# Cross-attention layer 0: probabilities cross PSUM two heads at a time over two adjacent banks, one bank for outputs, one for the rest, scaling on POOL, queries reloaded by batch

## The chip, the core and the metric

One NeuronCore of a Trainium2 chip runs the whole program; the metric is the device time of one launch in microseconds (us). Engines work from their own in-order queues and meet only at semaphores: TensorE (PE, with its weight loads PEld), VectorE (DVE), ScalarE (ACT), GpSimd (POOL) and SyncE (SP), whose queue here only issues DMAs.

## The reference, cut to what matters

Two layers follow each other on 8 batches of 112 tokens with a context of 375 rows; the change touches only the attention of the first layer, L0.

```python
def L0(x, ctx, mask):                       # x (8,112,512), ctx (8,375,512)
    q = (x @ Wq + bq)                       # 32 query heads of 16
    k, v = ctx @ Wk + bk, ctx @ Wv + bv     # 8 key/value heads of 16
    scores = q_head @ k_head.T / 4 + mask   # 112 x 375 for each (batch, query head)
    attn = softmax(scores)
    out = attn @ v_head                     # 112 x 16
    x = out @ Wo + bo + x
    return layernorm(x) * gamma + beta
# L1: two cross attentions (16 heads of 128), each with a layernorm and an output projection, then an MLP
```

## The kernel before

The batches are done in two halves of four (loop variable `hf`). A half is: a preparation (context and queries split in a high and a low fp32r part, keys, values and the first queries projected), the L0 attention, its output projection and layernorm, then eight groups of L1 attention and an MLP. In L1 every product is three matmuls (hi·hi, hi·lo, lo·hi; L652 to L654), and these fill most of the time.

**The L0 loop** runs over `n` = 0 to 127 heads of a half: `c` (four chunks of eight heads), in it `b` (four batches), in it eight heads. Step `n` writes these instructions on each engine:
- PE: three transposes of head `n`'s weights into a PSUM bank (`transpose0`, L784, recorded at L657), the scores of head `n+4` (`scores0`, L779), in some steps the projection of keys or queries (`L0_AT`), and for four heads together (a quad) six matmuls weights · values (`weigh0`, L802 to L805), the transposes of a finished quad (`four_transpose0`) and of a finished batch (`out_transpose0`).
- DVE: `max0(n+4)` (L1483: scores + mask to SBUF and their row maximum), then `lo_of` (L1318): transposed weights in PSUM minus their high part, 125x336, for head `n`; per quad `sum_outputs` (L1491, L1492); per eight heads (an octet) `scale_outputs` (L1499: 112x128, divides by the softmax sums) and `out0` (L1320).
- ACT: `move` (L1011) of the transposed weights of head `n` out of PSUM, rounded to the high part; `exps0(n+3)` (L1117); per quad `outputs` (33x448); per octet `out0` (L1013).

PSUM has eight banks. In L0 the loop uses two `scores`, two `tp` for transposes (by head, `n % 2`), `o_ps` and `pj2` for outputs (by quad), `pj0` and `pj1` (`aux`) in turn for everything else. `tp_free`, counted by `lo_of`, gates transpose `n+2`; `o_mid` gates the outputs bank; `aux_free` the aux banks.

**Queries and keys** pass through DRAM. Chunk `c+1`'s queries (448 columns, all four batches) replace chunk `c`'s in the tile `qo` by two DMAs of 64 partitions (`load_queries0(c, kv)`), each allowed only when the last heads that read its rows have been scored: after step 28 and 32 of the 32 heads of the chunk. Keys are reloaded batch by batch. The raw weights of the output projection and of L1's first group are loaded by SP between these and split on POOL in one piece, ahead of nothing else there.

## Time and profile before

| what | value |
|---|---|
| median of three runs (lowest, highest) | 2555.87 us (2555.66, 2564.72) |
| the profiled execution, its span | 2556.51 us, 2554.7 us |
| busy in the span: PE, PEld, DVE, ACT, POOL | 91%, 81%, 59%, 39%, 27% |
| L0 loop of half 0: first to last `max0` | 77.6 to 228.6 us |
| L0 loop of half 1: first to last `max0` | 1340.7 to 1489.8 us |
| granted TensorE clock, mean | 0.97 of full |

A row of the time line gives the start, the duration, engine, line and shapes of an instruction and, in brackets, how long the engine had idled and what released it. Durations overlap the next instruction's start, so the cost of an instruction in a stream is the step to the next start. A row of a table by stretch gives the stretch, its length and each engine's busy time in it.

### The profile page before, as it was taken

The numbers are of one execution on the slowest core, as the hardware profiler recorded it, in microseconds if no ns is written. First come the engines' busy times: TensorE is split into PE (matmuls) and PEld (weight loads), VectorE is DVE, ScalarE is ACT, GpSimd is POOL, SyncE is SP. The second block draws the span as 40 slices with busy tenths as digits, with TensorE's granted clock in tenths as the row PEclk, the third lists the DMA queues.
The fourth block names the chain that finished last, engine by engine and source line by source line (L and its number), as shares of the span: only waits on it lengthen the run. The fifth ranks groups of instructions, "written<-read, shape, count | busy, mean of one in ns | idle before, by whom it ended". The sixth has DMA issues, their size and how long they took to land. (4 is left out here: it accounts for less than half of the span.)

```text
span 2554.7 us, 36666 instructions
## 1 busy us (share of the span) xinstructions
PE 2329.4 (91%) x13176; PEld 2077.3 (81%) x13176; DVE 1506.3 (59%) x3426; ACT 998.7 (39%) x2271; POOL 698.1 (27%) x734
## 2 busy tenths in 40 slices
PE   4798799999999999998969978999999999999988
PEld 4565698999989898997756657999889898998976
DVE  4697655455575555456538976455555655455564
ACT  2686333332434333243118843342424333242420
POOL 4021213224141313313541211214141313314045
PEclk8899899999999999999989988999999999999999
DMA  5632222232333323223453412232323223223222
GB/s 184 203 113 61 66 87 92 88 103 84 104 99 92 100 75 104 88 91 127 149 160 103 111 49 68 90 95 88 102 94 102 92 79 103 86 91 116 77 69 81
DMA packets 118889, 253.25 MB, mean 99 GB/s; under 512 B 13648, under 2 KB 37232, under 8 KB 117664
## 3 DMA queue, kind: packets, MB, share of 16 engines
q1 hardware_dynamic: 76504, 140.73, 17.9%
q10 hardware_dynamic: 42208, 110.18, 14.0%
q8 instruction: 109, 1.79, 0.3%
q14 instruction: 68, 0.56, 0.1%
HBM read 222.40 MB, written 31.22 MB: 99 GB/s over the span
## 5 line engine op out<-in xcount | busy, mean ns | idle before, releaser
L652 PE MATMUL pj<-ctx_hi,wk_hi 128*128 128x376 f32 x1088 | 380.3, 350 | 36.5 <-DVE xacc L1369 21.6
L653 PE MATMUL pj<-ctx_lo,wk_hi 128*128 128x376 f32 x1088 | 372.7, 343 | 0.0
L654 PE MATMUL pj<-ctx_hi,wk_lo 128*128 128x376 f32 x1088 | 371.5, 341 | 0.0
L1318 DVE TENSOR_TENSOR rr<-pj,rr 128x448 fp32r<-128x448 f32 (+1 forms) x280 | 174.4, 628 | 249.5 <-ACT rr L1011 249.5
L576 POOL TENSOR_SCALAR wk_hi<-raw 128x512 fp32r<-128x512 f32 (+1 forms) x84 | 52.5, 625 | 977.6 <-DMA raw<-in_wk 817.8
L1320 DVE SCALAR_TENSOR_TENSOR k_lo<-pj,cur,k_hi 128x375 fp32r<-128x375 f32 x256 | 155.1, 607 | 247.2 <-ACT k_hi L1013 245.9
L657 PEld LDWEIGHTS tp<-ident,probs 112*125 112x125 f32 (+1 forms) x1536 | 197.9, 165 | 120.4 <-DVE probs L1598 41.9
L652 PE MATMUL pj<-pt_hi,nat 125*128 125x448 f32 x768 | 287.0, 374 | 7.0 <-issue 5.9
L657 PE MATMUL tp<-ident,probs 112*125 112x112 f32 (+1 forms) x1536 | 231.6, 270 | 60.2 <-DVE probs L1598 36.0
L1195 ACT ACTIVATE probs<-scores,prm 112x376 f32<-112x376 f32 x256 | 147.4, 576 | 353.2 <-DVE prm L1590 353.1
L1013 ACT ACTIVATE k_hi<-pj,cur 128x375 fp32r<-128x375 f32 x256 | 146.8, 573 | 353.1 <-PE pj L654 343.3
L654 PE MATMUL pj<-pt_hi,nat 125*128 125x448 f32 x768 | 282.5, 368 | 0.0
L653 PE MATMUL pj<-pt_lo,nat 125*128 125x448 f32 x768 | 282.2, 367 | 0.0
L652 PEld LDWEIGHTS pj<-ctx_hi,wk_hi 128*128 128x128 f32 x1088 | 211.4, 194 | 41.0 <-DVE xacc L1369 23.4
L576 POOL TENSOR_SCALAR wb_hi<-raw 128x512 fp32r<-128x512 f32 x152 | 98.1, 645 | 474.9 <-ACTq L1221 185.3
L1011 ACT ACTIVATE rr<-pj 128x448 fp32r<-128x448 f32 (+1 forms) x280 | 152.3, 547 | 162.0 <-PE pj L654 152.2
L653 PEld LDWEIGHTS pj<-ctx_lo,wk_hi 128*128 128x128 f32 x1088 | 211.3, 194 | 1.2
L654 PEld LDWEIGHTS pj<-ctx_hi,wk_lo 128*128 128x128 f32 x1088 | 210.8, 194 | 0.0
L578 POOL TENSOR_TENSOR wb_lo<-raw,wb_hi 128x512 fp32r<-128x512 f32 x152 | 200.6, 1320 | 12.7
L1318 DVE TENSOR_TENSOR pt_lo<-tp,pt_hi 126x336 fp32r<-126x336 f32 (+1 forms) x384 | 181.3, 500 | 10.0 <-ACT pt_hi L1011 10.0
L1011 ACT ACTIVATE pt_hi<-tp 126x336 fp32r<-126x336 f32 (+1 forms) x384 | 157.8, 448 | 46.6 <-PE tp L657 45.7
L652 PEld LDWEIGHTS pj<-pt_hi,nat 125*128 125x128 f32 x768 | 144.2, 188 | 27.5 <-issue 16.4
(168 smaller groups left out, 5326.9 us busy)
## 6 DMA issues: line engine op xcount, KB each, us to landing
nat<-nat_scratch ACTq DMA_DIRECT2D x256, 384.0 KB, 3.7
raw<-in_wk SPq DMA_DIRECT2D x72, 256.0 KB, 3.8
raw<-in_wq SPq DMA_DIRECT2D x72, 256.0 KB, 3.3
raw<-in_wo SPq DMA_DIRECT2D x72, 256.0 KB, 2.6
raw<-in_wv SPq DMA_DIRECT2D x64, 256.0 KB, 3.3
raw<-in_w SPq DMA_DIRECT2D x64, 256.0 KB, 2.9
nat_scratch<-rr SPq DMA_DIRECT2D x8, 1536.0 KB, 7.0
queries_scratch<-rr SPq DMA_DIRECT2D x32, 224.0 KB
```

The lines of the kernel that those rows point to most:

```text
L576: nc.gpsimd.tensor_scalar(hi, src, 1.0, 0.0, ALU.mult, ALU.add).then_inc(split_hi, 1)
L578: nc.gpsimd.tensor_tensor(lo, src, hi.bitcast(F32), ALU.subtract).then_inc(signal, k)
L652: nc.tensor.matmul(dst, l_hi, r_hi, start=first, stop=False)
L653: nc.tensor.matmul(dst, l_hi, r_lo, start=False, stop=False)
L654: return nc.tensor.matmul(dst, l_lo, r_hi, start=False, stop=last)
L657: return nc.tensor.transpose(dst, src, ident[0:parts, 0:parts])
L1011: i = nc.scalar.activation(dst, src, ACT.Copy)
L1013: i = nc.scalar.activation(dst, src, ACT.Identity, bias=bias)
L1195: nc.scalar.activation(probs[0:L, h, 0:SK], scores[n % SCR][0:L, 0:SK], ACT.Exp, bias=neg_max[0:L, h:h + 1], accum_out=row_sum[0:L, h:h + ...
L1318: i = nc.vector.tensor_tensor(dst, src, hi.bitcast(F32), ALU.subtract)
L1320: i = nc.vector.scalar_tensor_tensor(dst, src, bias, hi.bitcast(F32), ALU.add, ALU.subtract)
```

## The change

- **Two heads at once.** `tp0` and `tp1` become one tensor `tp_two` of two adjacent banks, `pj0` and `pj1` become `pj_two`. Heads are paired: the six transposes of a pair fill both banks of one of these (pairs take them in turn), then one `move` of 125x672 on ACT and one `lo_of` of 125x672 on DVE take both. New semaphores `two_ready`, `two_mid`, `two_free` count pairs; a pair's transposes wait for `lo_of` of the pair before the last.
- **Fewer banks for the rest.** Outputs have `o_ps` alone (`outputs` moves ahead of the `move` on ACT, and `weigh0` waits for `o_mid` of the quad before), all else has `pj2` alone.
- **Scaling on POOL.** `scale_outputs` leaves DVE for POOL; POOL's splits of the next weights are put between the scalings by twos, and their loads on SP move accordingly, with the copy of the second half's context now behind the four loads of `wo0`.
- **Queries by batch.** A chunk's queries come in eight DMAs of 64x4x112, two per batch, each pair as soon as the batch's heads of the chunk before are scored. `L0_AT` moves: keys 3 from step 9 to 5, queries from 15, 47, 79 to 12, 44, 76, in two steps instead of four.

```diff
-L0_AT = {1: ("k", 2), 9: ("k", 3), 15: ("q", 1), 47: ("q", 2), 79: ("q", 3)}
+L0_AT = {1: ("k", 2), 5: ("k", 3), 12: ("q", 1), 44: ("q", 2), 76: ("q", 3)}
-        o_banks, aux = (o_ps, pj[PJ - 1]), pj[0:NAUX]
+        twos, aux = (tp_two, pj_two), pj2
...
-                def load_queries0(c, kv):
-                    sp.wait_ge(q0_out, (hf * C0 + c + 1) * 64)
+                def load_queries0(c, b):
+                    if b == 0:
+                        sp.wait_ge(q0_out, (hf * C0 + c + 1) * 64)
                     if c > 0:
-                        sp.wait_ge(sc_ready, hf * SC_H + c * HB * HPC - 4 * (KV2 - 1 - kv))
+                        sp.wait_ge(sc_ready, hf * SC_H + (c - 1) * HB * HPC + (b + 1) * HPC)
+                    for kv in range(KV2):
+                        sp.dma_start(qo[64 * kv:64 * kv + 64, 4 * kv:4 * kv + 4, cols].bitcast(F32),
+                                     q_dram[hf, c, 4 * kv:4 * kv + 4, :, :, :, cols].rearrange("j r e d t -> (r e d) j t")
+                                     ).then_inc(q0_in[b], 16)
...
+                for i in range(NT // 8):
+                    scale_outputs(hf, i)
+                    if i in (3, 4):
+                        weights(base + RAW_W0, "o", hf * WO_H, hf * WO_H, chunks=range(2 * i - 6, 2 * i - 4))
+                    if i in (7, 8):
+                        keys1(0, range(2 * i - 14, 2 * i - 12))
+                    if i in (9, 10):
+                        queries1(0, chunks=range(2 * i - 18, 2 * i - 16))
...
                 def transpose0(n):
+                    two, i = divmod(n, 2)
                     pe.wait_ge(exp_ready, sc0 + n + 1 + SCR)
-                    pe.wait_ge(tp_free, tp0 + n + 1)
+                    if i == 0 and two >= 2:
+                        pe.wait_ge(two_free, two0 + two - 1)
...
-                        pe.wait_ge(tp_free, tp0 + 4 * u + 4 + TP)
-                        if u > 1:
-                            pe.wait_ge(o_mid, o0 + u - 1)
+                        pe.wait_ge(two_free, two0 + 2 * u + 2)
+                        if u > 0:
+                            pe.wait_ge(o_mid, o0 + u)
...
-                    move(pt0[n // 4 % 2][0][0:KC, n % 4, :], tp[n % TP][0:KC, 0:SC * L], tp_ready,
-                         tp0 + n + 1, mid=tp_mid)
+                    if n >= 8 and n % 4 == 0:
+                        outputs((n - 8) // 4)
+                    if n % 2 == 1:
+                        move(pt0[n // 4 % 2][0][0:KC, n % 4 - 1:n % 4 + 1, :], twos[two % 2][0:KC, :, 0:SC * L],
+                             two_ready, two0 + two + 1, mid=two_mid)
                     if n + 3 < NT:
                         exps0(n + 3)
-                    if n >= 8 and n % 4 == 0:
-                        outputs((n - 8) // 4)
...
-                        if n % 8 == 6:
-                            scale_outputs((n - 14) // 8)
```

On DVE, in the middle of the loop, the rows from one quad's sum to the next stood so before (L1483 is `max0`, L1318 `lo_of`, L1499 the scaling):

```order
184 L1492 TENSOR_REDUCE xacc<-pj 112x64
185 L1499 TENSOR_TENSOR xacc<-xacc,prm 112x128
186 L1483 ISA probs,prm<-scores,xacc 112x375
187 L1483 ISA prm 112x1
188 L1318 TENSOR_TENSOR rr<-tp,rr 125x336
189 L1483 ISA probs,prm<-scores,xacc 112x375
190 L1483 ISA prm 112x1
191 L1318 TENSOR_TENSOR pt_lo<-tp,pt_hi 125x336
192 L1320 SCALAR_TENSOR_TENSOR rr<-pj,prm,rr 128x112
```

and in the changed kernel, from the same place on:

```order
165 L1510 TENSOR_REDUCE xacc<-pj 112x64
166 L1501 ISA probs,prm<-scores,xacc 112x375
167 L1501 ISA prm 112x1
168 L1337 TENSOR_TENSOR rr<-pj_two,rr 125x672
169 L1501 ISA probs,prm<-scores,xacc 112x375
170 L1501 ISA prm 112x1
171 L1339 SCALAR_TENSOR_TENSOR rr<-pj,prm,rr 128x112
```

The scaling is gone from DVE, and one `lo_of` of 672 columns stands after every second `max0`.

On SP, the loads of the last chunk (keys and queries of L0, then the raw weights of L1's first group) before:

```order
44 L407 DMA k_hi<-keys_scratch 128x376
45 L422 DMA qo<-queries_scratch 64x4x448
46 L407 DMA k_hi<-keys_scratch 128x376
47 L422 DMA qo<-queries_scratch 64x4x448
48 L371 DMA raw<-in_wq 128x512 x4
```

and now:

```order
50 L412 DMA k_hi<-keys_scratch 128x376
51 L430 DMA qo<-queries_scratch 64x4x112 x2
52 L412 DMA k_hi<-keys_scratch 128x376
53 L430 DMA qo<-queries_scratch 64x4x112 x2
54 L376 DMA raw<-in_wq 128x512 x4
55 L412 DMA k_hi<-keys_scratch 128x376
56 L430 DMA qo<-queries_scratch 64x4x112 x2
57 L412 DMA k_hi<-keys_scratch 128x376
58 L430 DMA qo<-queries_scratch 64x4x112 x2
```

Each batch's queries follow its keys, and `wq` has moved from behind them to the middle.

## Rows read from the trace of the kernel before

**Rows 1.** Busy time by stretch: length; PE, PEld, DVE, ACT, POOL; clock, DMA
```profile
77.60:235.00 157.40, 142.29 (x901) 104.78 (x901) 138.80 (x481) 134.30 (x307) 22.88 (x24) 0.97 0.41 125
```
**Rows 2.** Same view for line 1483 alone, from one octet's first `max0` to the next
```profile
134.16:144.79 10.63, 4.39 (x16) 1.00 0.43 125
...
163.06:171.84 8.78, 4.39 (x16) 1.00 0.23 63
...
191.25:202.86 11.61, 4.42 (x16) 0.85 0.49 128
```
**Rows 3.** Time line of DVE in the L0 loop: start, duration, instruction, idle before
```profile
184.39 0.54 DVE L1483 CUSTOM_DVE_ANT_0 probs<-scores,xacc 112x375 f32<-112x375 f32 x1
...
184.85 0.50 DVE L1318 TENSOR_TENSOR rr<-tp,rr 125x336 fp32r<-125x336 f32 x1
185.27 0.17 DVE L1491 RECIPROCAL prm<-pj 112x4 f32<-112x4 f32 x1
...
185.73 0.29 DVE L1499 TENSOR_TENSOR xacc<-xacc,prm 112x128 f32<-112x128 f32 x1
185.94 0.54 DVE L1483 CUSTOM_DVE_ANT_0 probs<-scores,xacc 112x375 f32<-112x375 f32 x1
...
188.10 0.33 DVE L1320 SCALAR_TENSOR_TENSOR rr<-pj,prm,rr 128x112 fp32r<-128x112 f32 x1 [0.31 <-ACT rr L1013]
```
**Rows 4.** Time line of ACT in the same stretch
```profile
183.83 0.61 ACT L1117 ACTIVATE probs<-probs,prm 112x375 f32<-112x375 f32 x1
184.33 0.44 ACT L1011 ACTIVATE rr<-tp 125x336 fp32r<-125x336 f32 x1
184.66 0.61 ACT L1117 ACTIVATE probs<-probs,prm 112x375 f32<-112x375 f32 x1
...
187.30 0.53 ACT L1011 ACTIVATE xacc<-o_ps 33x448 f32<-33x448 f32 x1
187.72 0.34 ACT L1013 ACTIVATE rr<-pj,prm 128x112 fp32r<-128x112 f32 x1
```
**Rows 5.** Groups by line and shape, DVE: count, busy us, mean ns
```profile
L1318 DVE TENSOR_TENSOR rr<-pj,rr 128x448 fp32r<-128x448 f32 x256 | 159.2, 623 | 249.1 <-ACT rr L1011 249.1
...
L1318 DVE TENSOR_TENSOR pt_lo<-tp,pt_hi 125x336 fp32r<-125x336 f32 x128 | 64.4, 503 | 0.0
```
**Rows 6.** Time line of PE in the L0 loop
```profile
185.04 0.48 PE L657 MATMUL tp<-ident,probs 112*125 112x112 f32 x3
...
185.29 0.41 PE L779 MATMUL scores<-k_hi,qo 128*112 128x376 f32 x1
...
185.53 0.37 PE L802 MATMUL o_ps<-pt_lo,nat 125*17 125x448 f32 x1
...
185.74 0.36 PE L803 MATMUL o_ps<-pt_hi,nat 125*33 125x448 f32 x1
```
**Rows 7.** Time line of PE's weight loads at the last change of chunk
```profile
196.80 0.17 PEld L779 LDWEIGHTS scores<-k_hi,qo 128*112 128x112 f32 x1 [1.77 <-DMA qo<-queries_scratch]
```
**Rows 8.** Groups by line and shape, POOL
```profile
L578 POOL TENSOR_TENSOR wb_lo<-raw,wb_hi 128x512 fp32r<-128x512 f32 x152 | 200.6, 1320 | 12.7
...
L599 POOL TENSOR_TENSOR wk_lo<-raw,wk_hi 128x128 fp32r<-128x128 f32 x8 | 3.7, 461 | 0.7
```
**Rows 9.** Time line at the start of half 0's loop, SP's queue and DVE
```profile
68.70 1.41 SPq L422 DMA_DIRECT2D qo<-queries_scratch  x2
70.22 0.54 SPq L440 DMA_DIRECT2D xacc<-in_mask  x1
...
77.65 0.55 DVE L1483 CUSTOM_DVE_ANT_0 probs<-scores,xacc 112x375 f32<-112x375 f32 x1 [12.98 <-DMA xacc<-in_mask]
```
**Rows 10.** Time line of SP's queue at the start of half 1's loop
```profile
1334.60 3.21 SPq L398 DMA_DIRECT2D keys_scratch<-wk_lo  x4
1343.86 0.33 SPq L407 DMA_DIRECT2D k_hi<-keys_scratch  x1
```
**Rows 11.** DMA issues by line: count, KB each, median us to landing
```profile
ctx_copy<-in_ctx_t SPq DMA_DIRECT2D x1, 3000.0 KB, 13.6
```

More of the change, by code:

```diff
@@ L580, in split_free, with scale_outputs, weights @@
                 pool.sem_inc(raw_free[slot], 1)
-            def weights(n, name, free, use):
-                pool.wait_ge(w_free[name], free + 1)
-                for c in range(DC):
+            def scale_outputs(hf, i):
+                pool.wait_ge(o_inv, hf * O_H + 2 * i + 2)
+                pool.wait_ge(aux_free, hf * AUX_H + AUX_UNIT["four", 2 * i + 1] + 1)
+                nc.gpsimd.tensor_tensor(o_nat[0:L], o_nat[0:L],
+                                        inv_sum[0:L, :].unsqueeze(2).broadcast_to([L, HPC, HD0]),
+                                        ALU.mult).then_inc(o_nat_ready, 1)
+            def weights(n, name, free, use, chunks=range(DC)):
+                if chunks[0] == 0:
+                    pool.wait_ge(w_free[name], free + 1)
+                for c in chunks:
                     split_free(n + c, (1, GW), w_hi[name][:, c, :], w_lo[name][:, c, :], w_ready[name], 1,
@@ L809, in four_transpose0 @@
                 def four_transpose0(u):
-                    unit = AUX_UNIT["four", u]
                     pe.wait_ge(o_mid, o0 + u + 1)
-                    pe.wait_ge(aux_free, aux0 + unit + 1)
+                    pe.wait_ge(aux_free, aux0 + AUX_UNIT["four", u])
                     for h in range(4):
-                        last = transpose(aux[unit % NAUX][0:L, V0 * h:V0 * h + V0], o_t[:, h * L:(h + 1) * L], V0)
+                        last = transpose(aux[0:L, V0 * h:V0 * h + V0], o_t[:, h * L:(h + 1) * L], V0)
                     last.then_inc(aux_ready, 1)
                 def out_transpose0(i):
-                    unit = AUX_UNIT["batch", i]
                     pe.wait_ge(o_nat_ready, hf * C0 * HB + i + 1)
-                    pe.wait_ge(aux_free, aux0 + unit + 1)
-                    transpose(aux[unit % NAUX][:, 0:L],
-                              o_nat[0:L, :, :].rearrange("p h d -> p (h d)"), L).then_inc(aux_ready, 1)
+                    pe.wait_ge(aux_free, aux0 + AUX_UNIT["batch", i])
+                    transpose(aux[:, 0:L], o_nat[0:L, :, :].rearrange("p h d -> p (h d)"), L).then_inc(aux_ready, 1)
                 pe.wait_ge(pj_free, at["l0"] + PJ)
@@ L832, in _ @@
                     for step, name in L0_AT.items():
-                        unit = AUX_UNIT[name]
-                        place = name[1], aux[unit % NAUX], aux_ready, aux_free, aux0 + unit + 1
-                        if name[0] == "k" and n in (step - 1, step):
+                        if n in (step - 1, step):
                             i = 2 * (n - step + 1)
-                            keys0(*place, (i, i + 1))
-                        if name[0] == "q" and step - 4 < n <= step:
-                            queries0(*place, (n - step + 3,))
+                            make = keys0 if name[0] == "k" else queries0
+                            make(name[1], aux, aux_ready, aux_free, aux0 + AUX_UNIT[name], (i, i + 1))
                     if n >= 10 and n % 4 == 2:
@@ L1147, in _ @@
                         make = keys0 if name[0] == "k" else queries0
-                        make(name[1], aux[unit % NAUX], aux_ready, aux0 + unit + 1, aux_mid)
+                        make(name[1], aux, aux_ready, aux0 + unit + 1, aux_mid)
                     if n == 20:
@@ L1488, in sum_outputs @@
                     unit, at_h = AUX_UNIT["four", u], 4 * (u % 2)
-                    four = aux[unit % NAUX][0:L, 0:4 * V0].rearrange("p (h x) -> p h x", x=V0)
+                    four = aux[0:L, 0:4 * V0].rearrange("p (h x) -> p h x", x=V0)
                     dve.wait_ge(aux_ready, aux0 + unit + 1)
@@ L1505, in out0 @@
                     hi, lo = (o[:, c, b * L:(b + 1) * L] for o in ot0)
-                    lo_of(lo, aux[AUX_UNIT[name] % NAUX][:, 0:L], hi, aux_mid, am0 + AUX_MID[name] + 1, aux_free,
+                    lo_of(lo, aux[:, 0:L], hi, aux_mid, am0 + AUX_MID[name] + 1, aux_free,
                           bias=prm[:, PRM_C + 2 + 3 * c:PRM_C + 3 + 3 * c])
@@ L1514, in _ @@
                         max0(n + 4)
-                    lo_of(pt0[n // 4 % 2][1][0:KC, n % 4, :], tp[n % TP][0:KC, 0:SC * L],
-                          pt0[n // 4 % 2][0][0:KC, n % 4, :], tp_mid, tm0 + n + 1, tp_free)
+                    if n % 2 == 1:
+                        two = n // 2
+                        hi, lo = (p[0:KC, n % 4 - 1:n % 4 + 1, :] for p in pt0[n // 4 % 2])
+                        lo_of(lo, twos[two % 2][0:KC, :, 0:SC * L], hi, two_mid, two0 + two + 1, two_free)
                     if n in L0_AT:
```

97 lines of the change are left out of this document (42 added, 55 removed).

## The prediction

> **What bounds the kernel now.** I read the table by stretch first. In the L0 loop of half 0, PE is busy 142.3 of 157.4 us, DVE 138.8 and ACT 134.3 [rows 1]: three engines near 90%, at nearly full clock, where elsewhere PE alone is. The change can only act in the two L0 loops, about 150 us each, and at their ends. Then the same view for line 1483 alone, cut from one octet's first row maximum to the next. The undisturbed octet lasts 8.78 us; six of the fifteen in half 0 and seven in half 1 are within 0.3 us of that. The three octets with a query projection last 10.6 to 10.7; the one in which the last chunk of queries comes in lasts 11.61, at a granted clock of 0.85 [rows 2]. The time line says why 8.78. From start to start a `max0` costs DVE 0.46, a `lo_of` 0.42; the scaling holds it from 185.73 to 185.94 (0.21), after a gap behind the sums of the quad; `out0` is begun after 0.3 to 0.4 of waiting for ACT [rows 3]. With 0.27 per quad for the sums and 0.25 for `out0`, DVE's own work in an octet is 8 x 0.88 + 2 x 0.27 + 0.21 + 0.25 = 8.04; 0.7 is waits. ACT: `exps0` 0.50, `move` 0.33, `outputs` 0.42, `out0` 0.24 [rows 4]: 8 x 0.83 + 0.84 + 0.24 = 7.7. PE: three transposes 0.25, scores 0.24, a weigh pair 0.41 [rows 6], so 8 x 0.49 + 6 x 0.41, with 2 x 0.33 for the quad transposes and some 0.2 for the batch's (estimates of mine from the same engine's steps): 7.2. DVE is the bound, with ACT 0.3 behind and PE 0.8.
>
> **Part 1, pairs on DVE and ACT.** One `lo_of` of 672 columns replaces two of 336. From 448 to 336 columns the mean falls 623 to 503 ns, 1.07 ns a column [rows 5]; 336 columns more make the step 0.42 + 0.36 = 0.78 against 0.84. Per octet 4 x 0.06 = 0.24 less. On ACT the step is 0.33 at 336 columns and 0.42 at 448 [rows 4], 0.8 ns a column: 0.33 + 0.27 = 0.60 to 0.62 against 0.66, 0.2 less per octet. No row shows an access over two banks. If crossing cost nothing the saving is this; if each bank paid its whole fixed part again it is zero. A gain above it has no source. I take the first end, since the steps only stream columns.
>
> **Part 2, scaling on POOL.** DVE loses 0.21 and the gap of 0.2 before it. Its pure octet becomes 8.04 - 0.24 - 0.21 = 7.6, ACT's 7.5, PE's stays 7.2: no engine leads any more. POOL shows no 112x128 multiply; its nearest row is the two-input 128x128 subtract, 461 ns, the far one 128x512 at 1320 [rows 8]. DVE took 0.29 for its own [rows 3]. So 0.46, and between 0.29 and 1.3 as bounds. With a hand-over of 0.1 on each side, the batch transpose is released 0.66 after the sums instead of about 0.5. The Trainium skill, "GPSIMD Engine Reference", section "Performance versus the Vector engine", speaks against such a move: elementwise work belongs on DVE, as a tensor-tensor add measured 1.96 times slower on GpSimd. By that ratio the scaling would be an estimated 0.57, which would move an octet by 0.1 at most; no row here shows this very operation on POOL.
>
> **Part 3, the new cycle.** Pairing makes the hand-overs longer: a `move` lasts about 0.73 and a `lo_of` 0.85 before anyone may follow, 0.6 more than now on the way transposes, `move`, `lo_of`, `weigh0`. I walked two octets in the order of the code, with the steps above. The wait that ends last alternates: DVE stands about 0.3 before `out0`, because the one aux bank ties batch transpose, ACT's `out0` and DVE's `out0`; it stands 0.3 more before a `lo_of`, because PE, after `weigh0` has been freed by the previous pair, still has T, scores, quad transpose and weigh (0.25 + 0.24 + 0.33 + 0.41) ahead of the next pair's last transposes. 7.6 + 0.6 = **8.2** per octet against 8.78. Bounds: ACT's and DVE's pure 7.6 below; above, the 0.7 of waits of today plus 0.6 of longer hand-over on 7.6, 8.9. I take 8.2, and 24 octets: 24 x (8.78 - 8.2) = **-14**. The other eight: six hold a query projection, 12 matmuls of about 0.2, 2.4 us, now in two steps with the single aux bank. Today 1.87 of it shows, because PE had 1.5 to spare. After the change PE spares 1.0 and must wait for the quad's sums before and for both halves of the queries after, so I count these six at 10.6 as now. The first octet of each half takes both key projections instead of one: 0 over both octets.
>
> **Part 4, queries by batch.** In both halves the octets without a projection that exceed 8.78 do so by 7.0 in sum, the largest 11.61 - 8.78 = 2.8 [rows 2], where the scores' weights waited 1.77 for the queries [rows 7], and the clock fell with the idle PE. A batch's queries are now free 24 heads ahead of need, some 25 us, against a store and load of about 10. So **-7.0**.
>
> **Part 5, what SP issues at the start.** In half 0 DVE waits 13.0 us for the mask, and the mask is issued behind the query loads: two take 1.41 us of the queue, then the mask at 70.22 lands at 77.6 [rows 9]. Eight of them take 8 x 0.65 = 5.2 (each has as many pieces, a quarter as long), so the mask goes out 3.8 later. Its landing took 7.4 with the queries' bytes just ahead, which will then be mostly done: 1 may come back. **+3.0**, bounds +1.5 and +4.5. In half 1 the mask is early; the eight loads stand ahead of the second batch's key stores, so the load of these keys at 1343.86 [rows 10] moves to about 1347.7 and lands near 1350, where head 8's scores are wanted at 1349.5: **+1.0**, bounds 0 and +3.
>
> **Part 6, the other moved DMAs.** The copy of the context (3 MB, 13.6 us to landing [rows 11]) stood ahead of wo0's loads; it now comes behind all four, and the last two wait for POOL's splits after scaling 3, near head 42. The stores of chunk 2's queries follow at head 45 and queue behind its bytes: landed near head 56, reloaded near 60 to 61, where PE wants them at 58 to 59. **+2.5** in half 0, bounds 0 and +5. The splits between scalings hold POOL 2 x 1.95 = 3.9 of the 8 us until the next scaling, so they hide, as long as their raw data are there: `wq`'s at scaling 9 come about 3 late, and the split still ends 1 ahead of scaling 10.
>
> **Part 7, the ends.** The last pair's `move` and `lo_of` are 0.6 longer, the last scaling 0.3: +0.9 per half, **+1.8**.
>
> **The sum.** -14 - 7 + 3 + 1 + 2.5 + 1.8 = -12.7 on the profiled execution's 2556.5: 2543.8. That execution is 0.6 above the median of 2555.87, so I forecast **2543**. It is 0.5% below, which is the edge of what a measurement of this kernel can tell from no change; half of this case's chance lies on either side.
>
> **Rivals.**
> - *The pipeline closes up* (chance 0.20). Four banks hold four heads of transposes where two held two, so PE's waits for `lo_of` vanish, and octets run at DVE's 7.6 to 7.7. For it: PE's pure 7.2. Against: the walk finds PE behind `weigh0`. Price: 24 x 0.55 = -13 more, time 2530.
> - *Longer hand-overs eat the gain* (0.25). Octets at 8.5, as today's 0.7 of waits plus a bit on 7.6. Gain 24 x 0.28 = 7 and the 7 of part 4, less 8.3: 2550. That is no change.
> - *POOL and the single aux bank become the bound, slower* (0.17). Place: batch transpose, once per octet. PE waits for the scaling, ACT's and DVE's `out0` follow, and the quad transpose two steps later waits for the same bank. In the walk the release falls within 0.1 of the moment PE wants it; so each 0.1 beyond 0.66 adds nearly 0.1 to each of 32 octets. It outweighs the rest when the hand-over exceeds 0.66 by 12.7/32 = 0.4; at the far row's 1.3 in place of 0.46, it is 32 x 0.84 = +27, 2570. For: POOL's two-input row at 512 columns. Against: 461 at 128. A copy of the context that stalls a whole chunk would add to it.
> - *Banks are read one after the other at full cost* (0.05): part 1 falls, 32 x 0.24 = +8 on the forecast, 2551.
>
> The forecast has 0.33, and spans 2537 to 2549 by itself (octet 8.0 to 8.4). Range: from 2528 below, the first rival's time with a little more, to 2562 above, which leaves out the dearer half of the third. Faster by over 0.5%: 0.20 + half of 0.33 + some of the hand-over case = 0.43; slower by over 0.5%: 0.15; within: 0.42.
>
> **What would show it.** Octets of 8.2 from `max0` to `max0`, no 10.6 less than now in the three with a projection; `lo_of` steps of 0.78 and moves of 0.61 over two banks; no wait of scores for `qo` at heads 32 and 96, and one of 2 to 3 at head 64 of half 0; the first `max0` near 80.6 instead of 77.65; the scaling on POOL near 0.46. I am wrong if the multiply on POOL lasts over 0.8, if octets with no projection fall outside 7.9 to 8.5, or if the mask lands as early as now.

## The result, and the profile after

The changed kernel takes **2553.31 us**, median of 20 runs (2547.80 to 2555.72), the kernel before 2556.55 in the same comparison (20 runs, 2551.84 to 2564.72). The ratio is **0.9981, interval 0.9974 to 0.9989**: 0.2% faster, 4.9 us with 2.8 to 6.6 as bounds. The forecast was 2543, 0.5% faster. The time lies inside the range; the size is less than half of what was forecast. The profiled execution of the changed kernel took 2551.51 with a span of 2549.7, at a mean granted clock of 0.967; before it was 2556.51 and 2554.7.

The two L0 loops, from first to last `max0`, answer to [rows 1]. The stretch of [rows 1] runs 6 us past the loop, so the first line here is the kernel before again, cut at its last `max0` of half 0; the other two are the kernel after. Columns are the length, busy time of PE, PEld, DVE, ACT, POOL (instructions), granted clock, DMA share, GB/s.

```profile
77.65:228.65 151.00, 136.89 (x868) 101.53 (x869) 134.59 (x469) 130.35 (x298) 22.88 (x24) 0.97 0.43 130
...
81.46:226.50 145.04, 133.59 (x870) 103.95 (x871) 125.41 (x393) 124.32 (x236) 28.36 (x38) 0.98 0.43 131
1342.20:1485.49 143.29, 132.98 (x870) 103.12 (x870) 125.39 (x392) 124.27 (x237) 28.36 (x38) 0.99 0.35 101
```

Before, the same two stretches lasted 151.0 and 149.0. So the loops gave 11.7 us. In half 0 DVE was busy 89% of it before and ACT 86%; now both have 86%. PE has gone from 91% to 92%. The octets say where the time went. The same view for line 1501 (`max0`) alone, in half 0, answers to [rows 2].

```profile
111.51:119.83 8.32, 4.29 (x16) 1.00 0.55 147
128.15:137.77 9.62, 4.29 (x16) 1.00 0.19 57
137.77:147.71 9.94, 4.37 (x16) 1.00 1.00 322
147.71:157.24 9.53, 4.29 (x16) 1.00 0.47 155
193.57:202.63 9.06, 4.31 (x16) 1.00 0.49 134
```

An undisturbed octet is 8.32 instead of 8.78. The second and third row are the two that share a query projection: 19.56 together, where before an octet of 8.78 and one of 10.63 made 19.41. **Those pairs of octets gained nothing.** The fourth row is the octet from head 56, in which the queries of chunk 2 come in; the last one, from head 96, is a new stall.

DVE's time line through an undisturbed octet, answering to [rows 3] (start, duration, instruction, idle before and its releaser):

```profile
112.45 0.08 DVE L1501 DVE_READ_ACCUMULATOR2_ANT prm<- 112x1 f32 x1
112.60 0.86 DVE L1337 TENSOR_TENSOR rr<-tp_two,rr 125x672 fp32r<-125x672 f32 x1
113.38 0.54 DVE L1501 CUSTOM_DVE_ANT_0 probs<-scores,xacc 112x375 f32<-112x375 f32 x1
...
116.38 0.33 DVE L1339 SCALAR_TENSOR_TENSOR rr<-pj,prm,rr 128x112 fp32r<-128x112 f32 x1 [0.34 <-ACT rr L1030]
```

One `lo_of` of 672 columns moves DVE on by 113.38 - 112.60 = 0.78, the forecast's number. DVE stands 0.34 before `out0` (ACT's half comes late) and another 0.15 between the accumulator read, which starts at 112.45, and the pair's `lo_of`. The other side of the hand-over is on PE. The first line below is the kernel before, in the undisturbed octet of [rows 2]; the others are the changed kernel in another octet, with POOL's new instruction:

```profile
167.74 0.55 PE L657 MATMUL tp<-ident,probs 112*125 112x112 f32 x3 [0.46 <-DVE rr L1318]
...
185.40 0.39 PE L825 MATMUL o_ps<-pt_hi,nat 125*33 125x448 f32 x1 [0.33 <-DVE pt_lo L1337]
...
188.08 0.41 POOL L591 TENSOR_TENSOR xacc<-xacc,prm 112x128 f32<-112x128 f32 x1 [3.33 <-DVE xacc L1510]
```

Before, PE waited for `lo_of` to free a transpose bank: 52 such waits over both loops, 20.5 in all. With four banks there is none. In their place `weigh0` waits 0.33 for a `lo_of` that now covers two heads: 19 waits, 6.1 in all. POOL takes 0.41 for the scaling; the batch transpose on PE starts at 188.59, 0.10 after its end.

### The profile page after: what moved, and what is told of

Same layout as the page of the kernel before. It is cut to its first block and busy times, and to the rows that moved or that the text cites. A ratio compares the mean times of both kernels' runs of the same rounds, so it can differ in the third digit from the quotient of the medians.

```text
span 2549.7 us, 36311 instructions
## 1 busy us (share of the span) xinstructions
PE 2326.7 (91%) x13176; PEld 2086.6 (82%) x13176; DVE 1483.2 (58%) x3266; ACT 985.6 (39%) x2143; POOL 711.2 (28%) x766
## 5 line engine op out<-in xcount | busy, mean ns | idle before, releaser
L671 PE MATMUL pj_two<-ctx_hi,wk_hi 128*128 128x376 f32 x724 | 252.6, 349 | 28.2 <-DVE xacc L1388 21.4
L672 PE MATMUL pj_two<-ctx_lo,wk_hi 128*128 128x376 f32 x724 | 247.7, 342 | 0.0
L673 PE MATMUL pj_two<-ctx_hi,wk_lo 128*128 128x376 f32 x724 | 246.7, 341 | 0.0
L676 PE MATMUL tp_two<-ident,probs 112*126 112x112 f32 (+1 forms) x1152 | 163.5, 265 | 39.8 <-DVE probs L1608 39.7
L676 PEld LDWEIGHTS tp_two<-ident,probs 112*126 112x126 f32 (+1 forms) x1152 | 145.6, 159 | 59.5 <-DVE probs L1608 45.2
L671 PE MATMUL pj_two<-pt_hi,nat 125*128 125x448 f32 x462 | 171.9, 372 | 3.2 <-issue 2.4
L673 PE MATMUL pj_two<-pt_hi,nat 125*128 125x448 f32 x462 | 170.0, 368 | 0.0
L672 PE MATMUL pj_two<-pt_lo,nat 125*128 125x448 f32 x462 | 169.7, 367 | 0.0
L1134 ACT ACTIVATE probs<-probs,prm 112x375 f32<-112x375 f32 x256 | 148.0, 602 | 20.3 <-DVE prm L1501 19.6
L1608 DVE TENSOR_SCALAR probs<-probs,prm 112x376 f32<-112x376 f32 x256 | 147.6, 576 | 9.1
L1337 DVE TENSOR_TENSOR pt_lo<-tp_two,pt_hi 126x336 fp32r<-126x336 f32 (+1 forms) x288 | 144.1, 537 | 10.5 <-ACT pt_hi L1028 10.5
```

Source lines behind the costliest of these rows:

```text
L671: nc.tensor.matmul(dst, l_hi, r_hi, start=first, stop=False)
L672: nc.tensor.matmul(dst, l_hi, r_lo, start=False, stop=False)
L673: return nc.tensor.matmul(dst, l_lo, r_hi, start=False, stop=last)
L676: return nc.tensor.transpose(dst, src, ident[0:parts, 0:parts])
L1134: nc.scalar.activation(probs[0:L, n % 4, 0:S], probs[0:L, n % 4, 0:S], ACT.Exp, bias=neg_max[0:L, n % HPC:n % HPC + 1], scale=-1.0).then_i ...
L1337: i = nc.vector.tensor_tensor(dst, src, hi.bitcast(F32), ALU.subtract)
```

## The experiments

There were twelve runs: ten kernels, and the two of the comparison once more. The ratio is always to the kernel before, run beside them on the same chip; a kernel without a ratio had one execution, and its octets are what it was run for. Experiments 1 to 4 (but for the second kernel of 3) ran on one chip and 5 to 7 on another (but for the second kernel of 6); those two second kernels and experiment 8 ran on a third. So medians of different groups are compared only by their ratios. "Octet" is the time from one octet's first `max0` to the next, read as above.

### 1. Queries by batch, alone

The kernel before, with only `load_queries0`, its waits and its order among the key loads taken from the change:

```
-                    load_queries0(0, 0)
-                    load_queries0(0, 1)
+                    for b in range(HB):
+                        load_queries0(0, b)
...
-                        pe.wait_ge(q0_in[j // 4], (hf * C0 + c + 1) * 16)
+                        pe.wait_ge(q0_in[b], (hf * C0 + c + 1) * 32)
```

> The kernel before with one part alone: a chunk's queries come by batch (eight DMAs of 64x4x112 in place of two of 64x4x448), all else as before. Theory A (the waits for queries at the changes of chunk were worth 7 us over both halves, and the price is the mask issued 3.8 us later in half 0): from first to last row maximum 151.0 falls to 146.6 in half 0 and 149.0 to 146.4 in half 1, first row maximum of half 0 at 81.5 instead of 77.65, net about -3 us, 2553. Theory B (those waits were pulled out of slack that other waits take up again): the loops keep 151 and 149 to within 1, and the total is 4 slower, 2560.

Measured: 2557.34, ratio 0.9992 [0.9980, 1.0004]. Theory A holds for half 0, and for half 1 only in part. The octet of 11.61 [rows 2] is gone; in its place, for line 1481 of this kernel, columns as above:

```profile
194.64:203.43 8.79, 4.38 (x16) 1.00 0.60 159
```

Every undisturbed octet of half 0 but one (8.88) is within 0.02 of 8.78. The loops last 146.2 and 148.45 instead of 151.0 and 149.0. Half 1's first octet is 10.23 instead of 9.24: the forecast's +1.0 for its keys. Half 1 gave 0.6 where theory A had 2.6: two of its octets last 9.34 and 9.20, and in both DVE's scaling overlaps a split on POOL (experiment 3 shows what that does). The forecast had -7 + 1 for the loops; they show -5.4, and the ratio -2.0 with bounds of -5 and +1.

### 2. The pairs undone, on the same banks

The changed kernel, but each head is moved and subtracted by itself, and `two_free` counts heads:

```
-                    if n % 2 == 1:
-                        two = n // 2
-                        move(pt0[n // 4 % 2][0][0:KC, n % 4 - 1:n % 4 + 1, :], twos[two % 2][0:KC, :, 0:SC * L],
-                             two_ready, two0 + two + 1, mid=two_mid)
+                    move(pt0[n // 4 % 2][0][0:KC, n % 4, :], twos[n // 2 % 2][0:KC, n % 2, 0:SC * L],
+                         two_ready, two0 + n + 1, mid=two_mid)
```

> The changed kernel with pairing undone: the same four transpose banks, but each head's three transposes, its copy on ACT and its difference on DVE stand for themselves (336 columns), gated four heads back; outputs bank, aux bank, scaling on POOL, queries and splits as in the changed kernel. Theory A (the gain in an undisturbed octet, 8.78 to 8.32, comes from the fixed part of the pair instructions, 0.24 on DVE, and from the scaling gone from DVE, 0.2): octets of 8.55, +0.23 each, about +5 us in all against the changed kernel. Theory B (four banks give the gain, and pairing costs it back by longer hand-overs): octets of 8.1 or less, 3 to 5 us faster than the changed kernel.

Measured: 2550.96, ratio 0.9969 [0.9958, 0.9979]. Theory B: the undisturbed octet is **8.08, shorter than with pairs**. The first row is that octet, the other two are those with a projection (line 1497, columns as above):

```profile
117.92:126.00 8.08, 4.36 (x16) 1.00 0.47 132
126.00:135.76 9.76, 4.34 (x16) 1.00 0.19 57
135.76:145.45 9.69, 4.36 (x16) 1.00 0.94 314
```

DVE's time line in such an octet shows how:

```profile
1372.20 0.08 DVE L1497 DVE_READ_ACCUMULATOR2_ANT prm<- 112x1 f32 x1
1372.20 0.50 DVE L1333 TENSOR_TENSOR pt_lo<-tp_two,pt_hi 125x336 fp32r<-125x336 f32 x1
1372.84 0.33 DVE L1335 SCALAR_TENSOR_TENSOR rr<-pj,prm,rr 128x112 fp32r<-128x112 f32 x1
```

Here a `lo_of` follows its predecessor's accumulator read at once. The gap before `out0` is 0.22 (a `lo_of` step of 0.42 from 1372.20, then 1372.84), and it is the only one. Between first and last `max0` no `weigh0` on PE waits for `lo_of` any more, in either half. So DVE works 0.24 more per octet than with pairs (eight steps of 0.42 against four of 0.78) and waits some 0.5 less. The pairs save the work that the forecast counted, and lose twice that in waits.

### 3. The scaling back on DVE, with pairs and by head

Both kernels leave `scale_outputs` on POOL empty and call it on DVE behind the sums of each second quad; the first has pairs, the second is experiment 2's.

```
-                nc.gpsimd.tensor_tensor(o_nat[0:L], o_nat[0:L],
+                    nc.vector.tensor_tensor(o_nat[0:L], o_nat[0:L],
```

> The changed kernel with the scaling back on DVE (behind the second quad's sums, as before), POOL does only its splits, which no longer wait for scalings. Theory A (DVE is still the engine whose own work sets the octet): octets of 8.32 + 0.21 + a gap of 0.2 for its own sums = 8.7, about +10 us against the changed kernel. Theory B (the octet is set by the hand-overs from weigh to the last transposes, and DVE has 0.3 to spare before out0): octets of 8.35 to 8.45, +1 to +3 us. In both the stall at head 96, where the scaling waited behind POOL's split of wq, is gone (9.06 and 9.31 to 8.5).

> By head on four banks, as e2, with the scaling back on DVE. Theory A (by head, DVE's own work, 7.8 of the octet's 8.08, is what sets it, so the scaling costs its 0.21 in full, and its gap): octets of 8.3 to 8.45. Theory B (as with pairs, where it cost 0.08): 8.1 to 8.2.

Measured: with pairs 2553.31 (2561.17 in the profiled execution), ratio 0.9979 [0.9967, 0.9990], undisturbed octet 8.40: Theory B, POOL's scaling is worth 0.08 of an octet there. By head 2549.49 (one execution), 8.24 against 8.08, 0.16: between the two theories. An octet with pairs (they alternate between 8.38 and 8.41), and an octet by head:

```profile
118.58:126.96 8.38, 4.29 (x16) 1.00 0.46 137
```

```profile
156.69:164.93 8.24, 4.38 (x16) 1.00 0.40 121
```

On DVE the multiply lasts 0.29, on POOL 0.41. The 0.21 that it holds DVE isn't seen in full, because an engine that gets 0.21 less to do soon waits for another.

Both theories had said that the stall at head 96 would be gone. It isn't: the octet lasts 9.17 in half 0 and 8.70 in half 1 (by head 9.14 and 8.24). The reason there is another one. The two rows are POOL's split and DVE's scaling with pairs:

```profile
195.05 1.28 POOL L583 TENSOR_TENSOR wb_lo<-raw,wb_hi 128x512 fp32r<-128x512 f32 x1
...
195.36 1.12 DVE L1513 TENSOR_TENSOR xacc<-xacc,prm 112x128 f32<-112x128 f32 x1
```

DVE's multiply lasts 1.12 instead of 0.29 and ends 0.15 after POOL's instruction. The five kept traces with the scaling on DVE (the kernel before twice, experiments 1 and 3) hold 160 of these multiplies; 17 began while POOL worked and had over 0.15 of it ahead, and all 17 ended 0.13 to 0.15 after POOL, up to 1.18 long. `max0` and `lo_of` kept their lengths in such overlaps, 74 of them in the kernel before. So putting the scaling on POOL also does away with these collisions, which a mean over undisturbed octets doesn't show; no kernel was made to test that by itself.

With these the octet can be taken apart in three measured steps: the bank plan (by head, scaling on DVE) 8.78 to 8.24, **-0.54**; scaling to POOL -0.16, to 8.08; pairs **+0.24**, to 8.32. The parts of the bank plan (four banks for transposes, one each for outputs and the rest, `outputs` ahead of `move`) were not tried apart. What points at the first is that the waits of transposes for `lo_of`, 56 and 24.3 in all in experiment 1, are none in this kernel.

### 4. The mask first

In half 0 the load of the mask goes ahead of the queries' stores and loads in SP's queue:

```
+                    sp.wait_ge(pj_free, pre_freed("n", 2, SC - 1) + PJ)
+                    load_mask()
                     store_queries0(0, *pre_split("q", 0))
                     for b in range(HB):
                         load_queries0(0, b)
-                    sp.wait_ge(pj_free, pre_freed("n", 2, SC - 1) + PJ)
-                    load_mask()
```

> The changed kernel with the mask's load moved ahead of the first queries' stores and loads on SP in half 0. Theory A (only the mask held the start; the next that is late are the first batch's queries): first row maximum of half 0 near 73.5 instead of 81.47, total 7 to 8 us less than the changed kernel, 2546. Theory B (the bytes behind the mask, queries and two stores of 1.5 MB, set the start, or step 4's wait for those stores takes it up): first maximum near 77, or the first octet longer by what is won, total within 3 us of the changed kernel.

Measured: 2553.49, ratio 0.9980 [0.9968, 0.9993], as the changed kernel. Theory B, by its second clause. The first `max0` starts at 73.38, and the second octet lasts 17.01. The time line of ACT and of SP's queue:

```profile
74.20 0.60 SPq L388 DMA_DIRECT2D nat_scratch<-rr  x1
...
77.88 2.53 SPq L388 DMA_DIRECT2D nat_scratch<-rr  x1
```

```profile
89.99 0.61 ACT L1134 ACTIVATE probs<-probs,prm 112x375 f32<-112x375 f32 x1 [7.86 <-DMA nat_scratch<-rr]
```

From its step 4 on ACT needs the two stores of `nat`, which still stand behind the eight query loads; the `exps0` shown is the first one behind that wait. The wait only moved from the mask to them: whatever is last in that queue decides.

### 5. The moved DMAs and splits, later

The changed kernel, with the copy of the context behind the last query loads, and `wq`'s splits one octet later:

```
-                    if i in (9, 10):
-                        queries1(0, chunks=range(2 * i - 18, 2 * i - 16))
+                    if i in (10, 11):
+                        queries1(0, chunks=range(2 * i - 20, 2 * i - 18))
```

> The changed kernel with two transfers moved: the copy of the second half's context goes out behind the last queries of L0 instead of behind wo0, and POOL splits wq after scalings 10 and 11 instead of 9 and 10. Theory A (the stall at heads 56 to 72 of half 0 is queries queued behind the copy's 3 MB, the one at 96 to 104 is the scaling queued behind a split that waits for wq): octets at 56 and 64 fall from 9.53 and 8.45 to 8.35 each, the one at 96 from 9.06 and 9.31 to below 8.6; half 0's loop 145.0 to 143, half 1's 143.3 to 142.5. Theory B (both belong to the change of chunk itself): no octet moves by over 0.2.

Measured: 2548.85, one execution; the loops last 142.6 and 142.2 instead of 145.0 and 143.3. Theory A. The first row is the octet from head 56, 9.53 in the changed kernel, the second the one from head 96, 9.06 there. The octet from head 64 went from 8.45 to 8.31. In half 1, which has no copy, the octet from 96 went from 9.31 to 8.31, so that part is the splits' alone.

```profile
145.62:153.94 8.32, 4.29 (x16) 1.00 0.58 148
...
190.14:198.45 8.31, 4.29 (x16) 1.00 0.10 32
```

What stood there in the changed kernel, from its time line: the copy is issued at 136.04, ahead of the stores of chunk 2's queries (140.47), and their load is issued only at 153.31. At 156.79 the scores' weights have waited 1.78. The profile names no releaser for that wait; that it was these queries is read from the order and from this experiment. At head 96 POOL's split stood 4.72, its raw data having been asked for at 189.03, and the scaling queued behind it:

```profile
136.04 0.57 SPq L508 DMA_DIRECT2D ctx_copy<-in_ctx_t  x1
140.47 2.49 SPq L419 DMA_DIRECT2D queries_scratch<-rr  x4
...
153.31 1.30 SPq L430 DMA_DIRECT2D qo<-queries_scratch  x2
```

```profile
156.79 0.17 PEld L797 LDWEIGHTS scores<-k_hi,qo 128*112 128x112 f32 x1 [1.78 <-issue]
```

```profile
193.21 0.62 POOL L581 TENSOR_SCALAR wb_hi<-raw 128x512 fp32r<-128x512 f32 x1 [4.72 <-issue]
...
197.71 0.41 POOL L591 TENSOR_TENSOR xacc<-xacc,prm 112x128 f32<-112x128 f32 x1 [0.24 <-POOL wb_lo L583]
...
198.17 0.14 PEld L676 LDWEIGHTS pj<-ident,xacc 112*128 112x128 f32 x1 [1.37 <-POOL xacc L591]
```

### 6. The query projection, in three steps and cut to a third

Two kernels ask why an octet with a projection didn't get shorter. The first spreads its four groups of three matmuls over three steps instead of two:

```
+                        if name[0] == "q" and step - 2 <= n <= step:
+                            queries0(name[1], aux, aux_ready, aux_free, aux0 + AUX_UNIT[name],
+                                     ((0,), (1, 2), (3,))[n - step + 2])
```

> The changed kernel with each projection of queries spread over three steps (3, 6 and 3 matmuls in steps 11, 12, 13 of its place) instead of 6 and 6 in two. Theory A (the burst is what costs: PE holds back scores and transposes for 1.2 us twice, and ACT and DVE run dry): the two octets around it together fall from 9.63 + 9.93 to 19.2 or less. Theory B (the 2.4 us of matmuls and the wait for the one aux bank cost, however they are cut): 19.5 to 19.9, total unchanged.

The second leaves out the low parts in the loop's query projections, four of twelve matmuls remain, so the queries of chunks 1 to 3 are of lower precision:

```
-                        last = three(bank[:, 0:T], [w["b"][:, c, k * P:(k + 1) * P] for w in (w_hi, w_lo)],
-                                     (h_hi[:, c, :], h_lo[:, c, :]), c == 0, c == DC - 1)
+                            last = nc.tensor.matmul(bank[:, 0:T], w_hi["b"][:, c, k * P:(k + 1) * P],
+                                                    h_hi[:, c, :], start=(c == 0), stop=(c == DC - 1))
```

> The changed kernel with the three projections of queries inside the loop cut from 12 matmuls to 4 (high times high only; the low parts are left out): the same two steps, the same single aux bank, the same evictions. A projection costs 1.31 + 1.62 = 2.9 over undisturbed octets in the changed kernel, 1.87 before. Theory A (the matmuls show in full, 0.2 each): 2.9 falls by 8 x 0.2 = 1.6 to 1.3. Theory B (the waits for the single aux bank carry over half): it falls by 0.8 or less, to 2.1 or more.

The pair of octets in three steps (line 1503), and with a third of the matmuls (line 1505):

```profile
129.79:138.82 9.03, 4.29 (x16) 1.00 0.16 39
138.82:150.10 11.28, 4.39 (x16) 1.00 0.97 324
```

```profile
125.35:134.20 8.85, 4.30 (x16) 1.00 0.15 34
134.20:143.31 9.11, 4.38 (x16) 1.00 1.00 318
```

Three steps: 20.31, worse by 0.75 than the 19.56 of two and worse than either theory gave; 2554.95 in one execution. The projection then holds the single aux bank over one step more, and the quad transposes pay for it: behind each projection they wait 0.96 for DVE to free the bank, against 0.21 in the changed kernel, 5.8 against 1.2 over all six.

```profile
142.98 0.38 PE L676 MATMUL pj<-ident,xacc 33*112 33x33 f32 x4 [0.96 <-DVE rr L1341]
```

A third (2543.51 in one execution): 17.96, **1.60 less for 8 matmuls less**, exactly 0.20 each. Theory A: each matmul of the projection shows in full, none is hidden. Its cost over two undisturbed octets falls from 19.56 - 16.64 = 2.92 to 1.32, and 2.92 is the 12 x 0.2 of the matmuls and 0.5 of standing around them. The time line of the changed kernel in that place shows who stands, PE first: 0.48 ahead of the projection for the sums and 0.21 behind it for DVE, both to have the single aux bank. In the kernel before, with two aux banks, PE has no such wait at any of the six.

```profile
135.37 0.47 PE L671 MATMUL pj<-h_hi,wb_hi 128*128 128x448 f32 x1 [0.48 <-DVE xacc L1510]
...
137.29 0.54 ACT L1028 ACTIVATE xacc<-o_ps 33x448 f32<-33x448 f32 x1 [1.31 <-PE o_ps L825]
...
137.78 0.55 DVE L1501 CUSTOM_DVE_ANT_0 probs<-scores,xacc 112x375 f32<-112x375 f32 x1 [1.24 <-PE scores L797]
...
140.59 0.38 PE L676 MATMUL pj<-ident,xacc 33*112 33x33 f32 x4 [0.21 <-DVE rr L1339]
```

Six matmuls in a row hold PE for 1.2, and ACT and DVE run dry behind it by 1.31 and 1.24. More of the projection shows than before: 1.87 at an octet of 8.78 with two aux banks and four steps, 2.92 at 8.32 and 3.29 at 8.08 (9.76 + 9.69 - 16.16, experiment 2) with one bank and two steps. The last two share a bank plan and differ in the octet; between the first two both changed. The octet alone doesn't set it: with pairs and the scaling on DVE (experiment 3) it is 3.0 to 3.1 at 8.40. A kernel with two aux banks or four steps at the shorter octet was not tried.

### 7. The best of these together

By head on four banks, experiment 5's later DMAs, and at the start the mask **and both stores of `nat`** ahead of the first key and query loads; the second kernel adds the three steps.

```
-                    load_keys0(0, 0)
-                    load_keys0(0, 1)
                     store_queries0(0, *pre_split("q", 0))
-                    for b in range(HB):
-                        load_queries0(0, b)
                     sp.wait_ge(pj_free, pre_freed("n", 2, SC - 1) + PJ)
                     load_mask()
                     store_nat(0, 2, pre_freed("n", 2, SC - 1))
+                    store_nat(0, 3, pre_freed("n", 3, SC - 1))
+                    load_keys0(0, 0)
+                    load_keys0(0, 1)
+                    for b in range(HB):
+                        load_queries0(0, b)
```

> By head on four banks (as in e2), the DMA moves of e6, and at the start of half 0 the mask and both stores of natural values ahead of the first loads of keys and queries on SP. Theory A (with the stores out of the way step 4 does not wait 7.9 us for them): first row maximum of half 0 near 71, octets of 8.08, none of the first two octets over 11; loops 142 and 141.5; total 12 to 14 less than the changed kernel, ratio to before 0.993. Theory B (the 3 MB now delay the first queries by as much): first maximum at 77 or later, ratio 0.996.

> e9 with the projection over three steps. Theory A: as e9, with 0.3 to 0.5 less at each of six projections, 2 to 3 us in all. Theory B: the same as e9 within 1 us.

Measured: **2541.97, ratio 0.9920 [0.9906, 0.9934]**, faster than either kernel; with three steps 2543.18, 0.9929 [0.9917, 0.9942]. The loops last 140.0 and 139.8. With three steps they last 141.5 and 142.7, which neither theory had: a pair of octets with a projection takes 19.94 instead of 19.45, as in experiment 6. The octet from head 96 that had stalled (line 1497), and the start:

```profile
187.22:195.30 8.08, 4.34 (x16) 1.00 0.14 48
```

```profile
65.24 10.47 SPq L430 DMA_DIRECT2D qo<-queries_scratch  x8
```

```profile
77.87 0.94 PE L797 MATMUL scores<-k_hi,qo 128*112 128x376 f32 x2 [16.28 <-DMA qo<-queries_scratch]
78.65 0.55 DVE L1497 CUSTOM_DVE_ANT_0 probs<-scores,xacc 112x375 f32<-112x375 f32 x1 [13.12 <-PE scores L797]
```

The start went by Theory B, while the ratio beat both theories: the mask and `nat` no longer decide, now the queries do, whose eight loads took 10.47 to issue instead of 5.29. The first `max0` is hardly earlier, but nothing stalls in the octet behind it (10.67, against 17.01 in experiment 4).

### 8. Both kernels once more

> The changed kernel once more, for the time outside the L0 loops. Theory A (that time differs by chance, with the granted clock): from half 0's last row maximum to half 1's first one, 1115.7 in the first profile of the changed kernel and 1112.1 in that of the kernel before, some other value between 1110 and 1117. Theory B (the change makes L1 slower): 1115 or more again.

> The kernel before once more. Theory A: between 1110 and 1117. Theory B: 1112 or less again. Its L0 loops: 151.0 and 149.0 within 1.

One further profile of each: 2546.37 and 2569.51. What repeats and what doesn't is the use of them. Loops: after 145.2 and 142.7 (first profile 145.0 and 143.3), before 149.3 and 150.0 (151.0 and 149.0); in sum 287.9 against 299.3, the same 11 to 12 us. The first `max0` doesn't repeat: after 78.91 (81.47), before 80.82 (77.65). Nor does the time outside the loops, in which hardly an instruction changed: from half 0's last `max0` to half 1's first, before 1112.1 and 1115.9, after 1115.7 and 1112.5; from half 1's last `max0` to the end of the span, before 1065.0 and 1071.6, after 1064.2 and 1065.3. Two executions of the kernel before, on two chips, are thus 13 apart, all of it outside the loops.

## Why the prediction was wrong

**Where the forecast's loops missed.** Its terms made the two loops 17.5 shorter (-14 - 7 + 1 + 2.5); they are 11.7 shorter. Octet by octet the 5.8 come to the following, to within 0.3 (the last seven heads of a half are counted with the undisturbed octets):

| term | forecast | profile after | miss, both halves |
|---|---|---|---|
| undisturbed octet | 8.20 | 8.32 | +3.0 |
| each of six query projections, over undisturbed octets | 2.40 | 2.92 | +3.1 |
| scaling 10 behind `wq`'s split | 0 | 0.84 and 1.08 | +1.9 |
| queries behind the copy of the context | 2.5 | 1.34 | -1.2 |
| first octet of each half, with its keys | 9.41, 10.24 | 9.66, 9.04 | -1.0 |

**Part 1 and the total of part 3: right number, wrong source.** The step costs hold: 0.78 for a `lo_of` over two banks, 0.73 long for a `move`; crossing banks costs nothing. Octets fell to 8.32, inside the 8.0 to 8.4 that the forecast allowed itself, with the waits where the walk put them: 0.34 before `out0`, 0.33 at `weigh0`. But part 1 put down the pairs as a saving and said that a gain above it had no source. Experiment 2 shows that the pairs cost 0.24, and experiment 3 that the bank plan gives 0.54, with POOL's scaling 0.16 more. The sum could come out near right because part 3 charged the longer hand-overs to the same term. Its closeness is luck in that sense: a saving from the banks stood in no term. The source was named, but only in the first rival.

**The projections: the step that failed first.** In part 3, "I count these six at 10.6 as now" took 1.87 as the cost that shows and moved it up to 2.4, leaving 0.58 of gain in the neighbouring octet. Measured, the two octets that share a projection keep their time: 19.41 before, 19.57 after, 19.45 by head. Experiment 6 shows all 12 matmuls at 0.20 and some 0.5 of standing around them. The reasons given there were the right ones, PE's smaller spare and the single aux bank; together they were priced at 0.5 where they had to be priced at 1.1. The bank can be read off PE's rows: 12 waits around the six projections, 3.6 in all or 0.6 each, where the kernel before has none. How the rest divides between the shorter octet and the two steps in place of four stays open. Of 32 octets the forecast left eight without gain; the six projections alone took two each.

**The wq split: called hidden, and it wasn't.** Part 6 said that the split "still ends 1 ahead of scaling 10". It ended too late for it: POOL could begin at 193.21, two splits take 3.9, and the scaling came 0.24 behind the last one, at 197.71. Experiment 5 removes the stall by one octet's delay.

**The copy of the context: right.** Place and mechanism are those of part 6, for 1.34 instead of 2.5, inside its bounds. Other traces bear it out. In both kernels of experiment 3 POOL's splits wait for no scaling, the copy goes out 11 to 12 ahead of the stores instead of 4.4, and these two octets stall not at all. By head (experiment 2) they cost 3.07, with a third of the matmuls 4.33, where the stores came 2.8 behind the copy.

**Queries by batch: right mechanism, smaller gain.** The waits of [rows 7] are gone, and no octet waits for `qo` but the one behind the copy. Experiment 1 confirms that this edit alone levels the octets of half 0. Not all of the 7.0 was queries: in the octet of 9.10 of half 0 DVE's scaling lasts 0.79, held by POOL as in experiment 3. The price at the start comes next.

**The start, and what it costs the median.** In the profile the eight loads take 5.29 of SP's queue (forecast 5.2), the mask goes out at 74.48 instead of 70.22, and the first `max0` starts 3.8 later (forecast +3.0). These are SP's queue and DVE, answering to [rows 9]:

```profile
69.08 5.29 SPq L430 DMA_DIRECT2D qo<-queries_scratch  x8
74.48 0.53 SPq L449 DMA_DIRECT2D xacc<-in_mask  x1
```

```profile
81.47 0.55 DVE L1501 CUSTOM_DVE_ANT_0 probs<-scores,xacc 112x375 f32<-112x375 f32 x1 [14.82 <-DMA xacc<-in_mask]
```

One profile of each is not enough for this term, since the start alone differs by 2 to 3 between two executions of the same kernel. Over all kept profiles the first `max0` comes at 79.5 to 83.0 in the nine whose mask stands behind eight query loads, 80.8 in the mean, and at 77.65 and 80.82 in the two of the kernel before: 1.5 later, with much scatter. The other way is by medians: the change of the loops in each kernel's profile beside the change of its median by the ratio.

| kernel | loops | median | left |
|---|---|---|---|
| changed | -11.7 | -4.9 | 6.8 |
| 1, queries by batch | -5.4 | -2.0 | 3.4 |
| 2, by head | -13.1 | -7.9 | 5.2 |
| 3, scaling on DVE, pairs | -8.7 | -5.4 | 3.3 |
| 4, mask first | -6.2 | -5.1 | 1.1 |
| 7, best | -20.2 | -20.5 | -0.3 |
| 7, with three steps | -15.9 | -18.2 | -2.3 |

The four that issue the mask behind eight query loads lose 3.3 to 6.8 outside the loops, 4.7 in the mean; the three with the mask first -0.5. That looks like the 4.3 by which the mask goes out later, but the groups ran on different chips. On the chip of experiment 7 two kernels with the late mask (experiments 5 and 6, one execution each) lose only 1.6 and 1.2, in the mean 2.7 more than experiment 7's two. On the chip of experiments 1 to 4 the late mask loses 4.0, 2.9 more than experiment 4, though that one's first `max0` is over 6 earlier. So a price of 1.5 to 4 for the start fits what was measured, and the rest of what is lost outside the loops is not explained.

The two first profiles do close: start +3.8, loops -11.7, from half 0's last `max0` to half 1's first +3.7, after half 1 -0.7, together the -5.0 of the spans. The ends of the loops are in the last two; from the last `max0` to the last `out0` on DVE they take 0.86 and 0.81 longer, 1.7 where part 7 had 1.8. So the terms that the forecast had come to -11.7 + 3.8 + 1.7 = -6.2, and the 1.3 to the measured -4.9 are less than the 3.8 and 6.7 by which the two stretches outside the loops differ between two executions of the kernel before. In the L1 part one stretch with the same work (634 and 633 matmul and weight-load records) lasted 113.74 at a granted clock of 0.98 after and 112.09 at 1.00 before. Whether the change has a part in such dips stays open; the second profiles (1112.5 after, 1115.9 before) have them the other way round.

**POOL's scaling.** Forecast 0.46, measured 0.41; the slower-by-POOL rival falls. The Trainium skill's 1.96 ("GPSIMD Engine Reference", section "Performance versus the Vector engine") was measured for a large add; here POOL against DVE is 0.41 to 0.29, 1.4 times, and moving the work paid 0.08 to 0.16 an octet, since POOL was idle. In this kernel, where DVE is one of three engines near their limit and the operation is small, the rule to keep elementwise work on DVE would have cost that gain.

**The rivals.** "Longer hand-overs" (2550, octets of 8.5) is nearest to the median, yet for another reason: the hand-overs grew as the forecast itself had them, and the gain went to the projections, the splits and the start. Of "the pipeline closes up" the mechanism came true, since PE's waits for a transpose bank are gone, but its octet of 7.6 to 7.7 did not: the new wait at `weigh0` took their place, and without pairs the octet is 8.08.

## What to carry to other kernels

Before pairing two instructions into one wide one, price the extra buffers that the pairing brings by themselves: here the banks gave 0.54 an octet and the wide instructions took 0.24 back, because PE's `weigh0` and the output step waited for twice the work. When a steady loop gets faster or loses a spare bank, work that is now and then put into it loses its cover, so charge an inserted block at its full length on the busiest engine, and the waits for its bank on top. In a queue where several loads are waited for at the same moment, moving one to the front only hands the wait to the next; look at all that stand behind the long one, and place the ones with the earliest need first.

## What the runs showed of the hardware

- One instruction over two adjacent PSUM banks paid nothing for the crossing: 125x672 took 0.85 on DVE and 0.71 to 0.73 on ACT, each starting step in line with its columns.
- DVE's 112x128 multiply with both operands in SBUF lasted 0.29. Begun while a 128x512 instruction ran on POOL, it ended 0.13 to 0.15 after that one, up to 1.18 long (17 of 17 that began over 0.15 before POOL's end). `max0` and `lo_of`, which have one operand in PSUM, were not longer in the same overlaps.
- Issuing a DMA on SP's queue cost nearly the same for a quarter of the bytes with as many pieces: eight query loads took 5.29, 0.66 each, where two took 1.41, 0.70 each. In experiment 7 the same eight took 10.47, with the stores of `nat` and the key loads issued just ahead; what slowed them was not tried.
- In experiment 4 the granted clock over the first two octets was 0.73 and 0.80, and 1.00 in the third. PE had stood 12.85 for the first queries just ahead, and 4.76 more in the second octet, while ACT waited. Line 1501, columns as above:

```profile
73.37:82.63 9.26, 4.18 (x16) 0.73 0.87 278
82.63:99.64 17.01, 4.29 (x16) 0.80 0.48 155
99.64:109.55 9.91, 4.37 (x16) 1.00 0.48 143
```

```profile
72.60 0.94 PE L797 MATMUL scores<-k_hi,qo 128*112 128x376 f32 x2 [12.85 <-DMA qo<-queries_scratch]
...
90.65 0.76 PE L676 MATMUL pj_two<-ident,probs 112*125 112x112 f32 x2 [4.76 <-ACT probs L1134]
```
